# An expert's down product in high and low f32r parts, its sigmoid and gating one slot sooner, its weights in one buffer

## The reference

```python
xn = _layernorm(x)
# attention: 16 heads of 64; q, k, v with biases, softmax, output projection
out = x + attention(xn) + moe(xn)
# moe: router, top 8 of 64 experts, at most 128 tokens per expert
g = jnp.einsum('ecd,edf->ecf', xb, w_gate)      # 64 experts, 128 tokens, 256 -> 192
u = jnp.einsum('ecd,edf->ecf', xb, w_up)
h = jax.nn.silu(g) * u
y = jnp.einsum('ecf,efd->ecd', h, w_down)       # 192 -> 256, weighted and added to the tokens
# and a shared expert of the same shape for all tokens
```

## Time and profile before

| | |
|---|---|
| median of 3 runs | 3481.81 us (3479.49 to 3484.37) |
| the profiled execution | 3479.67 us |
| its span, first to last instruction | 3477.9 us |
| busy of the span: PE, DVE, ACT, POOL | 98%, 72%, 47%, 80% |
| mean granted PE clock | 0.992 |

### The profile page before, as it was taken

How to read it: one execution, slowest core, us unless ns; L and a number is a source line. 1 busy time by engine, 2 the same in 40 slices (tenths; PEclk the granted TensorE clock), 3 DMA queues, 4 the chain that set the end, 5 groups by cost and what they waited for, 6 DMA issues and landing times.

```text
span 3477.9 us, 61694 instructions
## 1 busy us (share of the span) xinstructions
PE 3402.9 (98%) x16978; PEld 2092.4 (60%) x16978; DVE 2511.5 (72%) x3133; ACT 1638.7 (47%) x3086; POOL 2796.8 (80%) x2378
## 2 busy tenths in 40 slices
PE   8999799999999999999999999999999999999988
PEld 6888555555555555555555555555555555555788
DVE  8999567777777777777777777777777777776555
ACT  4666344444444444444444444444444444444322
POOL 3433399999999999999999999999999999999322
PEclk9999899999999999999999999999999999999999
DMA  7887756777777767777767777777777777774676
GB/s 246 250 245 243 183 136 163 189 186 185 184 191 188 186 185 186 186 186 185 184 183 190 191 191 187 185 186 186 185 188 187 184 185 190 188 186 125 215 265 212
DMA packets 424338, 669.26 MB, mean 192 GB/s; under 512 B 63329, under 2 KB 228962, under 8 KB 424290
## 3 DMA queue, kind: packets, MB, share of 16 engines
q1 hardware_dynamic: 401506, 637.20, 66.9%
q0 software_dynamic: 14336, 23.08, 3.4%
q10 hardware_dynamic: 8448, 8.39, 0.7%
HBM read 306.98 MB, written 126.12 MB: 125 GB/s over the span
## 4 chain that ended last, share of the span: by engine, by line
PE 81%; DMA 3%; DVE 3%; issue 1%; SPq 1%; ACT 0%; POOL 0%; ACTq 0%; DVEq 0%; POOLq 0%
PE psum L1003 26%; PE psum L960 15%; PE psum L963 13%; PE psum L1064 10%; PE psum L988 10%; PE psum L1049 2%; DMA probs<-moe 2%; PE psum L1018 2%; PE psum L1168 1%; DVE k_rest L1483 1%; PE psum L1055 1%; PE psum L1056 1%; DVE merged L1356 0%; POOL probs L1641 0%; PE psum L1041 0%
## 5 line engine op out<-in xcount | busy, mean ns | idle before, releaser
L1265 ACT ACTIVATE probs<-psum 128x512 f32<-128x512 f32 x2048 | 1077.3, 603 | 1199.8 <-PE psum L963 1193.0
L1356 DVE TENSOR_REDUCE merged<-psum 128x1 fp32r<-128x1024 f32 x1024 | 1201.1, 1214 | 591.7 <-PE psum L988 582.4
L1610 POOL TENSOR_TENSOR sums<-sums,probs 128x512 f32<-128x512 f32 x762 | 973.6, 1278 | 60.1 <-ACT probs L1265 2.0
L1611 POOL TENSOR_TENSOR sums<-sums,probs 128x512 f32<-128x512 f32 x762 | 975.6, 1280 | 0.0
L1003 PE MATMUL psum<-probs,v_sb 128*64 128x512 f32 x4096 | 937.5, 600 | 0.0
L960 PE MATMUL psum<-q_full,k_full 128*128 128x512 f32 x2048 | 861.4, 421 | 2.5 <-DVE merged L1356 1.6
L963 PE MATMUL psum<-q_rest,k_rest 65*128 65x512 f32 x2048 | 811.7, 396 | 2.9 <-DMA q_rest<-turned 2.9
L1003 PEld LDWEIGHTS psum<-probs,v_sb 128*64 128x64 f32 x4096 | 271.7, 137 | 564.8 <-issue 497.0
L960 PEld LDWEIGHTS psum<-q_full,k_full 128*128 128x128 f32 x2048 | 388.1, 190 | 178.8 <-issue 76.8
L963 PEld LDWEIGHTS psum<-q_rest,k_rest 65*128 65x128 f32 x2048 | 389.8, 190 | 70.9 <-DMA q_rest<-turned 3.2
L1064 PE MATMUL psum<-x_t,w_qk 128*128 128x512 f32 x1536 | 407.3, 401 | 10.2 <-DVE merged L1356 5.8
(11 more groups left out here) (171 smaller groups left out, 3389.7 us busy)
## 6 DMA issues: line engine op xcount, KB each, us to landing
x_t<-xt SPq DMA_DIRECT2D x118, 1024.0 KB, 7.1
k_full<-high SPq DMA_DIRECT2D x256, 256.0 KB
v<-values SPq DMA_DIRECT2D x64, 512.0 KB, 3.3
w_qk<-wqk_parts SPq DMA_DIRECT2D x64, 512.0 KB
v_sb<-v SPq DMA_DIRECT2D x64, 512.0 KB, 5.6
q_full<-high SPq DMA_DIRECT2D x128, 256.0 KB
q_full<-low SPq DMA_DIRECT2D x128, 256.0 KB
k_rest<-low SPq DMA_DIRECT2D x128, 256.0 KB
```

Source lines behind the costliest of these rows:

```text
L1265: nc.scalar.activation(probs[:, kt, h, :], score_bank(j), ACT.Exp, scale=SCALE).then_inc(probs_ready, 1)
L1356: nc.vector.tensor_reduce(out=merged[:, q // GROUP, col:col + 1], in_=work[:, 2 * h:2 * h + 2, :].rearrange("p b c -> p (b c)"), axis=AX, ...
L1610: nc.gpsimd.tensor_tensor(total[:, 0, :], first[:, 0, :], probs[:, kt, 0, :], ALU.add)
L1611: nc.gpsimd.tensor_tensor(total[:, 1, :], first[:, 1, :], probs[:, kt, 1, :], ALU.add).then_inc(sums_added, 1)
```

## The change

- DN becomes five f32r matmuls: the hidden values and the down weights are each split in a high part (a copy to f32r) and a low part (the rest). Rows 128 to 191 of the hidden values lie in one tile as low part (partitions 0 to 63) and high part (64 to 127), so two of the five matmuls cover their terms.
- ACT makes the high parts: of the weights at the end of slot 0 (`split_down`, two copies), of the hidden values at the end of slot 2 (`split_hidden`, three copies). DVE makes the low parts: fillers WLOW (slot 2, behind `low_part`, two subtractions) and HLOW (end of slot 2, behind NORM1, two subtractions).
- SILU0 to SILU2 go from slot 2 to the end of slot 1, behind TOKEN2. POOL gates ahead of the first addition of the second half.
- The weights have one buffer, and are loaded later in SP's order, behind `store` half 0; the 64 rows of the second part are loaded twice, so there are four DMAs where there were three. Two DVE memsets at the start are left out, a smaller one is added.

```diff
 FILLERS = (((), (), ("RECIP0", "RECIP1")),
-           (("RECIP2", "RECIP3"), ("RAW1",), ("TOKEN0", "TOKEN1", "TOKEN2")),
-           (("NORM0", "SILU0"), ("SILU1", "SILU2"), ("NORM1",)),
+           (("RECIP2", "RECIP3"), ("RAW1",), ("TOKEN0", "TOKEN1", "TOKEN2", "SILU0", "SILU1", "SILU2")),
+           (("NORM0",), ("WLOW",), ("NORM1", "HLOW")),
            ((), ("RAW0",), ()))
...
-                pe.wait_ge(experts_loaded, 3 * DMA * (s + 1))
+                pe.wait_ge(gu_loaded, DMA * (s + 1))
...
-                pe.wait_ge(hidden_ready, s + 1)
-                nc.tensor.matmul(work[:, 1, 0:D], hidden[:, 0:P], w_d0[:, par, :], start=True, stop=False)
-                nc.tensor.matmul(work[:, 1, 0:D], hidden[:, P:2 * P], w_d1[:, par, :], start=False, stop=True
-                                 ).then_inc(dn_filled, 1)
+                pe.wait_ge(wd_low, s + 1)
+                pe.wait_ge(hid_low, s + 1)
+                terms = ((hid0[:, HIGH, :], wd0[:, HIGH]), (hid0[:, HIGH, :], wd0[:, LOW]),
+                         (hid0[:, LOW, :], wd0[:, HIGH]), (hid1[:], wd1[:, HIGH]), (hid1[:], wd1[:, LOW]))
+                for j, (tile, weights) in enumerate(terms):
+                    last = nc.tensor.matmul(work[:, 1, 0:D], tile, weights, start=(j == 0), stop=(j == len(terms) - 1))
+                last.then_inc(dn_filled, 1)
...
+        def split_down(s):
+
+            act.wait_ge(down_loaded, 3 * DMA * (s + 1))
+            if not known(s, 1):
+                act.wait_ge(dn_filled, s)
+            nc.scalar.copy(wd0[:, HIGH], w_d0[:])
+            nc.scalar.copy(wd1[:, HIGH], w_d1[:]).then_inc(wd_high, 1)
+
+        def split_hidden(s):
+
+            act.wait_ge(hidden_ready, s + 1)
+            nc.scalar.copy(hid0[:, HIGH, :], hidden[:, 0:P])
+            nc.scalar.copy(hid1[F2:P, :], hidden[0:F2, P:2 * P])
+            nc.scalar.copy(hid1[0:F2, :], hidden[0:F2, P:2 * P]).then_inc(hid_high, 1)
+
...
+                if g == 0 and att:
+                    split_down(s)
+                if g == 2 and att:
+                    split_hidden(s)
...
+            elif name == "WLOW" and att:
+                dve.wait_ge(wd_high, s + 1)
+                nc.vector.tensor_tensor(wd0[:, LOW], w_d0[:], f32(wd0[:, HIGH]), ALU.subtract)
+                nc.vector.tensor_tensor(wd1[F2:P, LOW], w_d1[F2:P], f32(wd1[F2:P, HIGH]), ALU.subtract
+                                        ).then_inc(wd_low, 1)
+            elif name == "HLOW" and att:
+                dve.wait_ge(hid_high, s + 1)
+                nc.vector.tensor_tensor(hid0[:, LOW, :], hidden[:, 0:P], f32(hid0[:, HIGH, :]), ALU.subtract)
+                nc.vector.tensor_tensor(hid1[0:F2, :], hidden[0:F2, P:2 * P], f32(hid1[0:F2, :]), ALU.subtract
+                                        ).then_inc(hid_low, 1)
...
-                    if (half, kt) == (1, GROUP - 1):
+                    if (half, kt) == (1, 1):
                         pool.wait_ge(silu_vec, 3 * s + 3)
+                        if not known(s, 1):
+                            pool.wait_ge(hid_low, s)
...
+        def load_down(p):
+            sp.dma_start(w_d0[:], io["w_down"][bass.ds(p, 1), 0:P, :].rearrange("o p d -> (o p) d")
+                         ).then_inc(down_loaded, DMA)
+            for half in (slice(0, F2), slice(F2, P)):
+                sp.dma_start(w_d1[half, :], io["w_down"][bass.ds(p, 1), P:F, :].rearrange("o p d -> (o p) d")
+                             ).then_inc(down_loaded, DMA)
...
             if fin:
                 store(s - 1, 0)
+            if nxt and att:
+                alone(sp, (standing, 1), (gu_loaded, DMA * (s + 1)), (gu_filled, s + 1),
+                      (down_loaded, 3 * DMA * (s + 1)), (wd_low, s + 1))
+                load_gate_up(p)
+                load_down(p)
             if nxt:
                 shift_out(s + 1, pp, 0)
```

More of the change, by code:

```diff
@@ L819, in attention_stage @@
     turned = sb("turned", [P, 2, BLOCK], F32R)
-    w_gu = sb("w_gu", [P, 2, KD, 2 * F])
-    w_d0 = sb("w_d0", [P, 2, D])
-    w_d1 = sb("w_d1", [P, 2, D])
+    w_gu = sb("w_gu", [P, KD, 2 * F])
+    w_d0 = sb("w_d0", [P, D])
+    w_d1 = sb("w_d1", [P, D])
+    wd0 = sb("wd0_e", [P, 2, D], F32R)
+    wd1 = sb("wd1_e", [P, 2, D], F32R)
+    hid0 = sb("hid0_e", [P, 2, P], F32R)
+    hid1 = sb("hid1_e", [P, P], F32R)
     count_slot = sb("count_slot", [P, 1], U32)
@@ L913, in attention_stage @@
     y_weighted = sem("y_weighted")
-    experts_loaded = sem("experts_loaded")
+    gu_loaded = sem("gu_loaded")
+    down_loaded = sem("down_loaded")
+    wd_high = sem("wd_high")
+    wd_low = sem("wd_low")
+    hid_high = sem("hid_high_e")
+    hid_low = sem("hid_low_e")
     slot_copied = sem("slot_copied")
@@ L1045, in item @@
                 pe.wait_ge(xt_copied, s + 1)
-                pe.wait_ge(experts_loaded, 3 * DMA * (s + 1))
+                pe.wait_ge(gu_loaded, DMA * (s + 1))
                 for c in range(3):
                     for kd in range(KD):
-                        last = nc.tensor.matmul(work[:, 1, c * P:(c + 1) * P], w_gu[:, par, kd, c * P:(c + 1) * P],
+                        last = nc.tensor.matmul(work[:, 1, c * P:(c + 1) * P], w_gu[:, kd, c * P:(c + 1) * P],
                                                 x_et[:, kd, :], start=(kd == 0), stop=(kd == KD - 1))
@@ L1125, in head @@
             table(E // 4, E // 2)
-            pe.wait_ge(set_up, 4)
+            pe.wait_ge(set_up, 3)
             pe.wait_ge(rows_out, 8)
@@ L1346, in _ @@
         nc.vector.memset(f32(merged[:]), 0.0).then_inc(set_up, 1)
-        nc.vector.memset(hidden[:], 0.0).then_inc(set_up, 1)
-        nc.vector.memset(w_d1[:], 0.0).then_inc(set_up, 1)
+        nc.vector.memset(f32(wd1[0:F2, LOW]), 0.0).then_inc(set_up, 1)
         nc.vector.memset(has[:, 0, :], 1.0).then_inc(has_ones, 1)
@@ L1694, in place, with load_gate_up @@
                              f32(high[head_rows, pp, 0, :]).rearrange("p (n c) -> p n c", c=HALF)).then_inc(placed, DMA)
[L1696 to L1703, removed]
+        def load_gate_up(p):
+            sp.dma_start(w_gu[:], one(io["w_gu"], p, "(k p) f", "p (o k) f")).then_inc(gu_loaded, DMA)
+        def load_down(p):
[4 more added lines that the diff above has]
+                             ).then_inc(down_loaded, DMA)
         def load_values(p, pp):
@@ L1709, in head @@
             load_values(0, 0)
-            load_expert(0, 0)
+            load_gate_up(0)
+            load_down(0)
             sp.wait_ge(lows_ready, 4)
@@ L1751, in step @@
                 if not known(s, 0):
[L1752 to L1759, removed]
                     waits.append((v_loaded, DMA * (s + 1)))
```

## The result

The changed kernel takes 3797.03 us (3795.84 to 3798.53) against 3483.09 us beside it: 1.0899 times as long, 95% interval 1.0884 to 1.0914. That is 314 us more. The forecast was 177 more, and the measured time lies above its range.

What follows compares the result with a forecast made beforehand. PE, busy for all 44.50 us of a step, was taken as the bound. Two stalls, 62 x (1.9 + 1.2) = 192.2, less 15.4 for DN, add 176.8 us: 3658.6 us for the median, range 3570 to 3755.

Steps and rivals of the forecast that it cites:

- The direction, the places and the releaser: Slower, chance 0.92, with PE idle ahead of PJ in slots 2 and 3, released by DVE's reductions.
- The product: DN on PE: five f32r matmuls take 0.62 us instead of 0.86, gaining 0.24 a step, 15.4 us in all.
- The first stall: PJ in slot 2 waits for quad 3's reduction behind the moved SILU: 1.9 us a step, bounds 1.0 to 2.3.
- The second stall: PJ in slot 3 waits for quad 5's reduction, delayed by WLOW and HLOW: 1.2 us a step, between 0 and 3.
- the rival with 0.09: Every DVE subtraction waits for its own POOL addition: 62 x (2.1 + 2.7) - 15 = 283, 3764 us; chance 0.09.
- with two 2.5: HLOW ahead of quad 5's reduction: if it waits for two POOL additions, the reduction is 2.5 us late.
- WLOW, which I thought needed cover: WLOW in slot 2: 1.6 us cover it; one POOL wait about fills that, two make reduce 4 some 1.2 late.
- The clock: Rival: the clock falls because PE idles; if each step lost 3 us to it, 3840 us; chance 0.03.
- but there the idle time was in one piece: Argument against a falling clock: the stage change idled in one piece, here two pieces of 1 to 2 us in 47.
- Part 4, the rest at nothing: ACT's copies, POOL's gating, SP's later weight DMAs, the single buffer and the memsets were all to cost nothing.

Runs made afterwards that it cites:

- e11: e8 with WLOW back on DVE, in idle times at the end of slot 3 and in slot 0, ACT splitting weights at slot 3's end; 3481.82 us.
- e1: The kernel before with only SILU0 to SILU2 moved behind TOKEN2 and POOL's gating moved earlier; 3558.99 us, ratio 1.0217.
- e7: The changed kernel with WLOW in slot 0 behind low_part and ACT's weight copies at the start of the step; 3813.57 us.
- e5: e6 with three unused reciprocals on DVE behind SILU2, to make PE idle ahead of PJ in slot 2; 3718.74 us.
- e4: The changed kernel with the four WLOW and HLOW subtractions on POOL and TOKEN0 to TOKEN2 ahead of reduce 2; 3549.73 us.
- e6: e4 with SILU0 moved ahead of reduce 2 and NORM1 moved ahead of reduce 4; 3558.04 us, ratio 1.0216.
- e8: e6 with POOL's HLOW subtractions one addition sooner; 3556.02 us, ratio 1.0208.

## Why the prediction was wrong

**The direction, the places and the releaser were right.** PJ in slots 2 and 3, behind a reduction that was already just in time; PE's new idle time is there and, but for 0.2 us a step ahead of quad 5, nowhere else.

**The product** was forecast at 0.62 us and took 0.60. Right as a term, 16 us of gain by the rows; no run has the 16 us in its time (e11).

**The first stall** was forecast at 1.9 us, within 1.0 to 2.3, and measured 1.13, by e1 as well: near the lower bound. I had named both opposing effects; the one that shrinks TOKEN0 (to 0.28) won, and SILU0 waited too, but only to 0.65.

**The second stall** is the first term that failed: 1.2 us, "one POOL addition more than is covered, the middle of what NORM1's waiting shows", against 2.26, and 0.2 more ahead of quad 5. The rule was right, an operation with two SBUF inputs ends with POOL's addition, but I took its waits as chances and averaged them. They aren't random. POOL adds without a break there and takes its turn after each of DVE's, so that HLOW's two wait for one each in nearly every step, 2.6 us together ahead of a reduction with 0.34 to spare. That was the rival with 0.09, and my own "with two 2.5". WLOW, which I thought needed cover, is nearly harmless next to it: without it in slot 2 the idle time in slot 3 is 1.85 instead of 2.10 (e7).

**The clock** is the second failure. It was a rival with a chance of 0.03 and priced at 3 us; the wrong step is "but there the idle time was in one piece". That was a misreading of the earlier trace rows: the timeline of PE in that very stretch of the kernel before has one piece of 5.84 us, then the full spacing of 0.23 again, then one of 2.45, and behind that one tile matmuls 0.42 us apart:

```profile
406.51 2.93 PE L1064 MATMUL psum<-x_t,w_qk 128*128 128x512 f32 x6 [5.84 <-DVE merged L1356]
...
411.84 0.40 PE L960 MATMUL psum<-q_full,k_full 128*128 128x512 f32 x1
412.08 0.39 PE L963 MATMUL psum<-q_rest,k_rest 65*128 65x512 f32 x1
...
416.05 0.73 PE L988 MATMUL psum<-high 64*128 64x512 f32 x4 [2.45 <-DVE merged L1356]
...
417.10 0.63 PE L963 MATMUL psum<-q_rest,k_rest 65*128 65x512 f32 x1
417.52 0.63 PE L960 MATMUL psum<-q_full,k_full 128*128 128x512 f32 x1
```

So it could have been seen beforehand that a piece of 2.45 us is enough; e5 shows it for 2.1. In the step shown, slot 3 lost 3.64 us, of which 2.26 is idle time; with the 0.26 that DN is shorter, 3.64 - 2.26 + 0.26 = 1.64 us belong to the lower clock (some 0.1 of it to PE's restart). Over all steps the 209 us at half speed cost 104, 1.7 a step.

Together, for 62 steps: 1.13 for the first stall, 0.3 for quad 5 and PE's restart, 2.26, 1.64, less 0.26, makes 5.07 a step and 314 us, which is what was measured. Against the forecast's 177 that is 62 x 1.06 = 66 us more for the second stall, 62 x 1.64 = 102 for the clock, 19 for quad 5 and the restart, and 62 x 0.77 = 48 less for the first stall. The clock is the largest of the errors; with it right and all else as forecast the sum would have been 3760, with the second stall right alone 3724.

**Part 4, the rest at nothing,** held for the change: ACT's copies, SP's order and the single buffer show up in no wait of PE. (One count in it is wrong: the 14 us from shift_out to the next step's first tile held for its old place, so a shift_out 5 us later would have had 9.) What it overlooked is POOL. I counted its 3.5 us as room; e4 to e11 show that some 2 of them can't be had.

## What to carry to other kernels

Where an engine is only just in time, price an insertion ahead of it by what it takes in that place, not by its columns: a DVE operation with two SBUF inputs beside a POOL that never stops costs one whole POOL operation each, here 1.35 us where the same subtraction alone took 0.28, and two in a row cost two; in e7 some cost two each. Then add what the idle time itself costs on PE, by its length: 1 us cost no clock here, 1.4 us cost it one time in seven to eleven, and 2.1 us cost 1.7 more in most steps. And a stall that moves when it is removed (e4, e6, e8) points at an engine that is full; look at the step's length before the next place is mended.

## What the runs showed of the hardware that I had not expected

- DVE and POOL mostly alternate over such operations, but not strictly. NORM1 took 0.69, 1.63 and 2.65 us in different kernels, with the same work, by where it met POOL's additions; the last waited for two of them.
- It isn't only operations with two SBUF inputs. TOKEN0 and SILU0 have one, and took 0.28 or 1.12 and 0.28 to 0.94 us by where they met an addition; the pair of reciprocals behind SILU0 took 1.75 to 1.77 us in all of these kernels, though POOL was adding.
- Lengthening works both ways: the addition that NORM1 got ahead of took 1.81 instead of 1.28.
- PE's clock fell to half behind most idle times of 2.1 us between dense stretches, at a cost of 1.7 us or so each, behind a few of 1.3 to 1.5, and behind none of 1.0. The Trainium skill (TensorE: Matmul & The Clock Gate, "Why this matters for your kernels") warns only of idle gaps between bursts of matmuls that are longer than any of these. In e5 2.1 us were enough, where nearly all of PE's idle time in a step is this one wait, and the measurement decides.
